# Attention and ternary FFN layer on one core: both fronts reordered, output projection made directly in natural layout

## The reference

```
q, gate = split(x @ Wq);  k = x @ Wk;  v = x @ Wv        # 8 query heads, 2 key heads, D = 64
q, k = partial_rope(q), partial_rope(k)                  # on 16 of the 64 dimensions
o = softmax(q k^T / 8) v;   x = norm(x + (o * silu(gate)) @ Wo)
w(W) = ternary(W / s) * s,  s = mean |W| per row         # FFN weights 256 -> 1024 -> 256
h = x @ w(Wfc)^T + g * (x @ v^T @ fast_b^T @ u^T);   x = norm(x + relu(h)^2 @ w(Wproj)^T)
```

## Time and profile before

| | us |
|---|---|
| median of 3 runs (1678.25 to 1680.78) | 1679.8 |
| the profiled execution | 1687.55 |
| its span in the trace | 1685.7 |
| TensorE busy in it | 1622.7 (96%) |
| VectorE busy | 1357.7 (81%) |
| GpSimd busy | 1023.0 (61%) |
| ScalarE busy | 738.5 (44%) |

### The profile page before, as it was taken

The page is one execution under the profiler, slowest core; times in us unless marked ns, Lnnn a source line. Parts: engine busy times, 40 slices in busy tenths (PEclk is TensorE's granted clock), DMA queues, the critical chain, the costliest instruction groups (busy, mean ns, idle before and its releaser), DMA issues.

```text
span 1685.7 us, 21033 instructions
## 1 busy us (share of the span) xinstructions
PE 1622.7 (96%) x6902; PEld 808.8 (48%) x6902; DVE 1357.7 (81%) x1677; ACT 738.5 (44%) x1406; POOL 1023.0 (61%) x784
## 2 busy tenths in 40 slices
PE   6899999999999999999988999999999999999997
PEld 2544444444444444447754444444444444444676
DVE  7888888888888888757886888888888888886577
ACT  1344444444444444444423444444444444444333
POOL 7466666666666665653475566666666666656233
PEclk8899999999999999999998999999999999999998
DMA  6311111111111100020052111111111111000101
GB/s 204 92 30 25 24 24 24 24 25 26 26 26 26 26 22 4 1 94 25 14 149 58 24 24 24 24 24 25 24 24 24 24 24 24 20 1 1 38 25 38
DMA packets 38428, 58.26 MB, mean 35 GB/s; under 512 B 6736, under 2 KB 17632, under 8 KB 38320
## 3 DMA queue, kind: packets, MB, share of 16 engines
q1 hardware_dynamic: 36016, 53.63, 12.2%
q10 hardware_dynamic: 2304, 3.30, 0.8%
HBM read 18.50 MB, written 4.19 MB: 13 GB/s over the span
## 4 chain that ended last, share of the span: by engine, by line
PE 85%; DVE 8%; issue 2%; DMA 2%; POOL 1%; SPq 1%; ACT 1%; DVEq 0%; POOLq 0%; ACTq 0%
PE ob L665 27%; PE trio L653 17%; PE trio L654 13%; PE sc L618 9%; PE trio L588 7%; PE sc L734 3%; PE trio L767 2%; PE trio L676 2%; PE ob L782 1%; PE trio L782 1%; DVE oge L1408 1%; DMA wqg_sb<-in_wq 1%; DVE acc L362 1%; DVE qb L1429 1%; DVE stats L1362 1%
## 5 line engine op out<-in xcount | busy, mean ns | idle before, releaser
L362 POOL TENSOR_TENSOR acc<-acc,probs 128x512 f32<-128x512 f32 x448 | 578.6, 1291 | 391.7 <-DVE acc L362 387.4
L988 ACT ACTIVATE probs<-trio 128x512 f32<-128x512 f32 x1024 | 529.5, 603 | 603.4 <-PE trio L654 583.5
L1294 DVE TENSOR_REDUCE maxp<-sc 128x2 f32<-128x1024 f32 x472 | 575.0, 1218 | 140.3 <-PE sc L620 138.5
L665 PE MATMUL ob<-probs,v_sb 128*64 128x512 f32 x2048 | 496.2, 605 | 0.0
L362 DVE TENSOR_TENSOR acc<-acc,probs 128x512 f32<-128x512 f32 x448 | 402.8, 899 | 61.8 <-ACT probs L988 55.6
L653 PE MATMUL trio<-qa,kab 128*128 128x512 f32 x1024 | 439.9, 430 | 3.6 <-DMA qb<-mrow 2.4
L654 PE MATMUL trio<-qb,kab 128*128 128x512 f32 x1024 | 405.8, 396 | 0.0
L653 PEld LDWEIGHTS trio<-qa,kab 128*128 128x128 f32 x1024 | 192.5, 188 | 284.3 <-issue 211.7
L665 PEld LDWEIGHTS ob<-probs,v_sb 128*64 128x64 f32 x2048 | 124.0, 136 | 242.4 <-issue 173.6
L654 PEld LDWEIGHTS trio<-qb,kab 128*128 128x128 f32 x1024 | 194.2, 190 | 23.9
L618 PE MATMUL sc<-kab,qa 64*128 64x512 f32 x512 | 192.9, 453 | 12.6 <-DVE maxp L1438 7.0
(11 more groups left out here) (126 smaller groups left out, 1439.4 us busy)
## 6 DMA issues: line engine op xcount, KB each, us to landing
qa<-high_sb SPq DMA_DIRECT2D x120, 128.0 KB, 2.3
qb<-low_sb SPq DMA_DIRECT2D x64, 128.0 KB, 2.4
tables_sb<-in_tables SPq DMA_DIRECT2D x36, 128.0 KB, 2.5
xT_sb<-in_xT SPq DMA_DIRECT2D x8, 512.0 KB, 5.4
acc<-in_x SPq DMA_DIRECT2D x8, 512.0 KB, 4.2
out_y<-acc SPq DMA_DIRECT2D x8, 512.0 KB, 3.0
rot_sb<-raw_sb SPq DMA_DIRECT2D x72, 32.0 KB, 1.9
kab<-acc SPq DMA_DIRECT2D x16, 128.0 KB, 2.9
```

Of the source, the lines that this page charges most:

```text
L362: ops.tensor_tensor(total, total, part, ALU.add).then_inc(summed, 1)
L665: mm = nc.tensor.matmul(ob[hd * D:(hd + 1) * D, :], v_sb[:, t, kv * D:(kv + 1) * D], probs[:, t % RING, hd * CHUNK:(hd + 1) * CHUNK], star ...
L988: nc.scalar.activation(probs[:, t % RING, hd * CHUNK:(hd + 1) * CHUNK], score_bank(t, hd), ACT.Exp, scale=float(D) ** -0.5).then_inc(probs ...
L1294: nc.vector.tensor_reduce(two_columns(p, j), MAX_PAIRS[j % 2], AX_X, ALU.max).then_inc(maxed, 1)
```

## The change

**First front.** The fourth chunk of x is loaded one place earlier and Wproj later, behind the big transfer of Wqg. k3's projection goes ahead of the low-rank product, whose result ScalarE copies to SBUF. The second half of the Wfc preparation leaves the front: `above_less_below` and the sum with the low-rank product become `prepare_wfc`, behind the front's reductions; all of Wproj's preparation goes into unit 0; Wfc's four groups of transposes go into units 1 and 2, Wproj's into 3 and 4, the scale row into 5. The passes for maxima no longer stand behind q1's projection and the Wfc preparation.

**Second front.** VectorE rotates q0 ahead of the last second sum; ScalarE rounds k0 and q0 ahead of the copies of k1 and k2; the last chunk's statistics and norm come after the first four reductions instead of ahead of them, and its store later on SyncE. Slot 3 moves to `qa`, out of the store's buffer.

**Batch end.** The output projection swaps its operands: 16 matmuls with 256 moving columns, in natural layout, replace 8 with 512, their copies and 8 transposes per chunk. Chunk 1's goes to `ob` and `misc`.

```diff
-        high = [high_sb[:, i, :] for i in range(2)] + [acc_halves[:, i, 0, :].bitcast(F32R) for i in range(2)]
+        high = [high_sb[:, i, :] for i in range(2)] + [acc_halves[:, 0, 0, :].bitcast(F32R), qa[:, PAIRS - 1, 0, :]]
...
+        def projected(c, i):
+            if c == 1:
+                return (ob if i < 2 else misc)[:, (i % 2) * HID:(i % 2 + 1) * HID]
+            return sc[:, 2 + i // 2, (i % 2) * HID:(i % 2 + 1) * HID]
...
                 front_rest(0, b)
+                if b == 0:
+                    sp.dma_start(wp_nat, w_proj.rearrange("(h p) j -> p h j", p=P)).then_inc(wp_loaded, 16)
+                if b >= 1:
+                    store(b * NCH - 1)
                 front_tables(5, b)
...
-                for h in range(HC):
+                if c == 1:
+                    pe.wait_ge(o_copied, done((n // NCH + 1) * UNITS))
+                    pe.wait_ge(den_used, done((n // NCH + 1) * UNITS))
+                else:
+                    pe.wait_ge(res_done, done(n * TILES))
+                for i in range(TILES):
                     for p in range(PAIRS):
-                        mm = nc.tensor.matmul(sc[:, h, :], wo_sb[:, p, h * P:(h + 1) * P],
-                                              og[:, c * PAIRS + p, :], start=(p == 0), stop=(p == PAIRS - 1))
-                    mm.then_inc(attn_ready, 1)
+                        mm = nc.tensor.matmul(projected(c, i), og[:, c * PAIRS + p, i * P:(i + 1) * P], wo_sb[:, p, :],
+                                              start=(p == 0), stop=(p == PAIRS - 1))
...
                 front_project(3, b)
+                front_project(4, b)
                 if b == 0:
                     setup_low_rank()
-                front_project(4, b)
-                front_project(5, b)
-                if b == 0:
-                    pe.wait_ge(setup_dve, 1)
+                    pe.wait_ge(setup_act, 2)
...
                     front_round(0, b)
+                    front_round(1, b)
+                    front_copy(2, b)
+                    front_copy(3, b)
+                    front_round(2, b)
                     deviation(2 * b * NCH - 1)
-                    front_round(1, b)
-                    front_round(2, b)
                     front_copy(4, b)
...
+            def prepare_wfc():
+                for j in range(JT):
+                    last = above_less_below(wfc_w[:, j, :], wfc_nat[:, j, :], j)
+                link(last)
+                dve.wait_ge(setup_act, 2)
+                for j in range(JT):
+                    last = nc.vector.scalar_tensor_tensor(
+                        out=wfc_w[:, j, :], in0=wfc_w[:, j, :], scalar=full[:, j:j + 1],
+                        in1=low_rank_w[:, j, :], op0=ALU.mult, op1=ALU.add)
+                last.then_inc(setup_dve, 1)
...
+                    if b == 0 and first(c, p) and y == 2:
+                        prepare_wp_thresholds()
+                    if b == 0 and first(c, p) and y in (3, 4):
+                        prepare_wp_below(y - 3)
+                    if b == 0 and first(c, p) and y in (5, 6):
+                        prepare_wp_above(y - 5)
...
                 for i in range(PASSES):
+                    if b >= 1 and i == TILES:
+                        variances(2 * b * NCH - 1, y2)
+                        second_norm(b * NCH - 1, 2 * b * NCH - 1)
                     front_reduce(0, i)
...
-    if b == 0 and c == 0 and y in (4, 5) and 2 * (p - 1) + y - 4 in range(5):
-        return 2 * (p - 1) + y - 4
-    return None
+    group = 2 * (c * PAIRS + p - 1) + y - 4
+    return group if b == 0 and y in (4, 5) and group in range(9) else None
```

More of the change, by code:

```diff
@@ L457, in front_rest, with store @@
                 place_rest(front(s), b, k_rest(n) if what == "k" else q_rest(n))
+            def store(n):
+                sp.wait_ge(post_done, done(n + 1))
+                sp.dma_start(out_tiles[:, n, :, :], yout).then_inc(y_stored, 16)
             def front_begin(b):
@@ L531, in _ @@
                         load_residual(c + 2)
-                    sp.wait_ge(post_done, done(n + 1))
-                    sp.dma_start(out_tiles[:, n, :, :], yout).then_inc(y_stored, 16)
+                    if c < NCH - 1 or b == BATCH - 1:
+                        store(n)
             sp.wait_ge(y_stored, 16 * (BATCH * NCH + 1))
@@ L777, in ffn_down @@
                         pe.wait_ge(y2_done, done(n * TILES))
+                    if j == 0 and n % NCH == 0:
+                        pe.wait_ge(res_done, done((n + 2) * TILES))
                     pe.wait_ge(sq_split, done(n * JT + j + 1))
@@ L1011, in step @@
                 return emit
-            def copy_attention(n):
-                act.wait_ge(tr_ready, done(2 * n))
-                for h in range(HC):
-                    act.wait_ge(attn_ready, done(n * HC + h + 1))
-                    nc.scalar.copy(attnT[:, h, :], sc[:, h, :]).then_inc(attn_copied, 1)
             def deviation(count):
@@ L1051, in front_round @@
                 what, n = FRONT[s][0:2]
-                if b >= 1 and s == 1:
+                if b >= 1 and s in (1, 3):
                     act.wait_ge(ffn2_ready, done(2 * b * NCH))
@@ L1070, in _ @@
                     front_copy(4, b)
+                    setup_low_rank_copies()
                     front_round(2, b)
-                    for g in range(4):
-                        setup_wfc_copy(g)
                     front_round(3, b)
+                    front_round(4, b)
                     front_copy(5, b)
-                    front_round(4, b)
                     copy_v(0, b)
@@ L1257, in _, with prepare_wp_thresholds @@
             link(last)
-            for j in range(JT):
-                last = above_less_below(wfc_w[:, j, :], wfc_nat[:, j, :], j)
-            link(last)
-            dve.wait_ge(setup_pe, 2)
-            for j in range(JT):
-                last = nc.vector.scalar_tensor_tensor(
-                    out=wfc_w[:, j, :], in0=wfc_w[:, j, :], scalar=full[:, j:j + 1],
-                    in1=sc[:, j // 2, (j % 2) * HID:(j % 2 + 1) * HID], op0=ALU.mult, op1=ALU.add)
-            last.then_inc(setup_dve, 1)
-            def prepare_wp_below():
+            def prepare_wfc():
[8 more added lines that the diff above has]
+                last.then_inc(setup_dve, 1)
+            def prepare_wp_thresholds():
                 dve.wait_ge(wp_loaded, 16)
@@ L1271, in prepare_wp_below @@
                 thresholds(slice(JT, JT + HC), wp_nat, FFN)
-                for h in range(HC):
-                    last = below(wp_w[:, h, :], wp_nat[:, h, :], JT + h)
-                    nc.vector.tensor_scalar(wp_scale[:, h * P:(h + 1) * P], ident[:, :],
-                                            full[:, JT + h:JT + h + 1], None, ALU.mult)
-                link(last)
+            def prepare_wp_below(h):
+                dve.wait_ge(setup_dve, 1)
+                nc.vector.tensor_scalar(wp_scale[:, h * P:(h + 1) * P], ident[:, :],
+                                        full[:, JT + h:JT + h + 1], None, ALU.mult)
+                link(below(wp_w[:, h, :], wp_nat[:, h, :], JT + h))
             def prepare_wp_above(h):
@@ L1350, in _ @@
             LN_LINKS = 2 * TILES + 2
-            WP_LINKS = 4
-            setup_links = chain[0] + WP_LINKS
+            LATE_LINKS = 6
+            setup_links = chain[0] + LATE_LINKS
             def variances(count, src):
@@ L1386, in residual_add @@
                     if i % 2 == 0:
[L1387 to L1389 removed]
+                        dve.wait_ge(attn_ready, done(2 * n + i // 2 + 1))
+                    nc.vector.tensor_tensor(y1[:, i, :], projected(n % NCH, i), xres[:, i, :], ALU.add)\
+                      .then_inc(res_done, 1)
             def first_stats(n, count):
@@ L1447, in _ @@
                 if b == 0:
-                    prepare_wp_below()
+                    prepare_wfc()
+                dve.wait_ge(y_stored, 16 * (NCH * b + 1))
                 attention_cycles(dve, step(b))
```

157 lines of the change are left out of this document (66 added, 91 removed).

## The result

| | median us | runs | ratio to the kernel before, 95% interval |
|---|---|---|---|
| before | 1683.18 | 15 | |
| changed | 1686.96 | 15 | 1.0025 [1.0015, 1.0035] |
| changed, once more (`after_again`) | 1688.14 | 8 | 1.0035 [1.0014, 1.0056] |

The kernel became 4 to 6 us slower. (0.1% is 1.7 us throughout.

What follows compares the result with a forecast made beforehand. TensorE was 85% of the chain, so gains were sought where it waits: the fronts and batch ends. The terms -7.5 + 1.2 - 3.2 - 1.4 + 1.7 + 1.4 + 0.2 gave -7.6 us, a median of 1672.2 us, range 1664 to 1678.5.

Steps and rivals of the forecast that it cites:

- The first front, -7.5 forecast: First front into unit 0: TensorE starts attention 13 us earlier, VectorE is free 8 us earlier, unit 0 ends 7.5 us earlier.
- VectorE free at 66, 8 us earlier than 74.09: Before unit 0: reductions reach 58, `prepare_wfc` takes 8 us, so VectorE is free at 66 instead of 74.09.
- unit 0 becomes VectorE's: Unit 0: VectorE, with 5.1 us idle, gets 5.6 us of Wproj's preparation; the unit ends 7.5 us earlier.
- More groups in units, +1.2: Units 1 to 4: four groups of transposes join at 0.3 us each, +1.2 us.
- The batch ends, -1.5 in sum (-3.2, -1.4, +1.7, +1.4): Batch ends: transposes between chunks -3.2, batch 1's earlier transposes -1.4, lower clock +1.7, projections +1.4 us.
- the charge for the lower clock: Batch 0's end: TensorE idles 3 us instead of 1.13 and may then run at its lower level, +1.7 us.
- The second front, +0.2 forecast: Second front: last reduction at 885.7 to 887.2, where the next pass waited until 887.10 before; +0.2 us, ends -4 and +6.
- +6 (the norm not covered at all): Second front: the slow end of its charge, VectorE's norm of the last chunk not covered at all, +6 us.
- q1's transfer still deciding its end: Second front: a sign to look for in the changed profile, q1's transfer still setting the front's end.
- q1 does not come earlier: Second front: k3's copy stands behind the deviation and q1's row swap late on SyncE; part of the +0.2 us charge.
- The one on the slow side: Rival before unit 0: GpSimd stays busy beside `prepare_wfc`, all sixteen instructions take 20.5 us; 1684.7 us, slower; chance 0.06.

Runs made afterwards that it cites:

- e_above: Against the kernel before: batch end and first front changed, but the eight above-less-below instructions back ahead of the first reduction; 0.9983 of before.
- e_c: The kernel before with the batch-end part alone, both fronts as before; 0.9999 [0.9988, 1.0010] of before, median 1679.28 us.
- e_best: The changed kernel with above-less-below, statistics and norm put back, q1's row swap and the row of maxima earlier; 0.9978 of before, median 1677.98 us.

## Why the prediction was wrong

**The first front, -7.5 forecast, +2.1 found** (111.6 - 109.5 over the traces). The step that failed is "VectorE free at 66, 8 us earlier than 74.09", with what followed for unit 0. Three errors of 3 to 3.5 us each:
- The starting point. 74.09 was one execution's value, the latest of seven; their mean is 70.6. Taking the difference off the median did not mend that, since it is the difference that was too large: 3.5 us.
- `prepare_wfc` began at 59.73 and not at 58, and took 9.4 us where 8 were charged; over three traces VectorE was free at 69.0, not 66: 3.0 us.
- Unit 0 takes 42.5 us from VectorE's first reduction; 39.5 was forecast (66 to 105.5), before it was 38.9: 3.0 us. The part of Wproj's preparation that moved there costs VectorE 7.1 us (2.8 for the thresholds, twice 0.39 + 1.78), not 5.6. The 128x1024 comparison alone went from 0.75 us in its old place, with GpSimd idle, to 1.78 beside a rotation of GpSimd's. And the sum let this work fill VectorE's 5.1 us of idle time, but VectorE is still idle for 5.1 of the 42.5 us, 4.4 of them in and right behind TensorE's stretch at the lower clock. Without that stretch the unit takes 41.8 us in `e_above`, so the stretch is worth about 0.7 of the 3.0.

The front itself was right: first reduction 32.2 for 31, row of maxima 56.4 for 54.6, attention 58.5 for 56.6. But TensorE's 9 to 11 us were worth nothing, as VectorE set the end. The text said that unit 0 becomes VectorE's; it did not say that the moved work had stood in idle time, where it cost nothing. `e_above` shows it: half of it back, and 6.6 us return.

**More groups in units, +1.2:** right. The stretch from the end of unit 0 to that of unit 4 takes 169.6 us instead of 168.8, and unit 5 42.1 instead of 41.8.

**The batch ends, -1.5 in sum (-3.2, -1.4, +1.7, +1.4):** `e_c` measured 0, with an interval of -2.0 to +1.7 us, so the sum may be right but was too small to be seen. The transposes are the 0.85 us above; the charge for the lower clock is there as well. The two other terms were mis-sized: the transposes of batch 1 came 0.8 us earlier, not 1.4, and a chunk's projections took 7.07 us for 32 records where 16 took 7.03 in the same place, so 0.2 us in sum and not 1.4. From unit 31 on, the two traces of before took 134.1 and 131.7 us, twelve with the change 131.4 on average.

**The second front, +0.2 forecast, +2.8 to +3.6 found.** That lies between the value chosen and the named end "+6 (the norm not covered at all)". The failed step is "q1's transfer still deciding its end" taken as "q1 does not come earlier": it came 2.9 us later. Everything needed stood in the paragraph (k3's copy behind the deviation, the swap behind the store), but no price was put on it. q1's swap left SyncE at 878.29 for 875.46 in before: k3's copy came 2.6 us later (868.75 for 866.17) and its swap 1.4, the store took 0.59, and the issues of q0's rest took 3.6 us instead of 2.6. VectorE's part came as forecast in this one execution (887.01). In the three other traces with the change's second front the last maximum comes 1.8 to 3.1 us later, counted from the projection of k1, and TensorE's projection of q2 takes 2.4 to 3.3 us there instead of 2.0; so VectorE's chain lost time as well.

**The rivals.** The one on the slow side named the right engine and the wrong cost. GpSimd did run beside `prepare_wfc`, for three rotations as the forecast said, and the sixteen took 9.4 us, not 20.5. What made the kernel slower is the sum of two mechanisms that the text priced at their favourable values; 0.06 for the slow side was too low with a term of -7.5 that rested on one execution's 74.09.

**The sum again:** +2.1 +1.2, +2.8 to +3.6, and 0 to -1.5 for the batch ends make 4.6 to 6.9 us, against 4.2 and 5.9 measured.

## What to carry to other kernels

Before work is moved off an engine's list, look at what that engine did meanwhile: the preparation stood in idle time of VectorE, and clearing the way for TensorE put it on the path, for an engine that was the next bound. When two chains end within 3 us of each other, price both for every reordering; an edit that frees one shows only the gap to the other, and it took edits on both, together (`e_best`), to win. And a difference of a few microseconds must not start from one execution: take the point that it hangs on from several traces.

## What the runs showed of the hardware

**Contention went the other way round.** In the earlier trace rows VectorE's instructions with both inputs in SBUF took 1.28 us each beside GpSimd. In the changed kernel the first eight of them took 0.40 each (3.23 for eight), and GpSimd's rotation, begun 0.06 us after the first of them, took 4.31 us instead of 1.27; the next eight took 0.78 each. `e_above` shows the same pair, 3.23 and 4.30. The Trainium skill, "SBUF — State Buffer", section "SBUF: two separate sides", says that of a VectorE instruction with two SBUF inputs and a GpSimd instruction that reads SBUF, whichever starts first holds the shared port pair for its whole instruction while the other blocks; the trace agrees in who loses (the later one). In these rows the later one also waited through a whole train of eight instructions, not one.

**Same order, different time.** Seven executions of the same first front end unit 0 between 108.1 and 113.0 us. q1's projection, which waits for the transfer of Wqg in all seven, starts between 33.5 and 36.6 us, the transfer itself takes 10.3 to 12.6 us, and the stretches of lower granted clock fall in different places, as in the windows above. That is larger than most terms of the prediction's sum.
